# A four-batch adaLN, attention and expert-adapter layer on one core: set-up of the weights and of the first rows rewritten, 64 matmuls put first on TensorE

## The reference, cut to what matters

```python
mod = (silu(c) @ wmod).reshape(4, 6, 1, -1)
sa, ca, ga, sb, cb, gb = (mod[:, i] for i in range(6))
ga = (2 * (ga >= 0) - 1) * max(abs(ga), 0.25)          # gb the same
h = layernorm(x) * (1 + ca) + sa
x = x + ga * attention(h)      # layernorm(h)*gamma+beta -> q, k, v -> causal softmax -> o_proj, + h
h = layernorm(x) * (1 + cb) + sb
x = x + gb * ffn(h)            # silu(gate) * up, 704 wide, with rank-16 adapters of the top 2 of 8 experts
```

## Time and profile before

| | us |
|---|---|
| median of 3 executions | 689.21 (688.83 to 689.48) |
| the profiled execution | 688.73 |
| its span, first to last instruction | 686.9 |
| TensorE matmul busy | 652.9 (95%) |
| VectorE, GpSimd, ScalarE busy | 474.2, 377.4, 356.7 |

### The profile page before, as it was taken

One profiled execution on the slowest core, in us unless ns is written; L12 is line 12 of the kernel. 1 busy time (PEld: TensorE's weight loads), 2 busy tenths in 40 slices (PEclk: granted clock), 3 DMA queues, 4 the chain that ended last, 5 costly groups with the idle time before them and its releaser, 6 DMA issues.

```text
span 686.9 us, 10710 instructions
## 1 busy us (share of the span) xinstructions
PE 652.9 (95%) x3772; PEld 558.8 (81%) x3772; DVE 474.2 (69%) x1146; ACT 356.7 (52%) x642; POOL 377.4 (55%) x473
## 2 busy tenths in 40 slices
PE   4869999999999999999999999999999999999996
PEld 3559987888879987888878897798888998788885
DVE  5997678478886677658976767747987657637323
ACT  4635455546455546465455446564454546654543
POOL 3785345538577236647576516654765635543644
PEclk9989999999999999999999999999999999999999
DMA  8300020000000020000000001000000000000000
GB/s 311 122 1 1 1 62 0 1 2 31 0 2 31 1 62 0 1 1 32 0 1 32 1 1 62 0 1 18 15 1 1 32 1 1 0 1 1 31 0 32
DMA packets 14054, 15.45 MB, mean 22 GB/s; under 512 B 1328, under 2 KB 12720, under 8 KB 14000
## 3 DMA queue, kind: packets, MB, share of 16 engines
q1 hardware_dynamic: 14000, 14.76, 6.4%
HBM read 10.57 MB, written 4.19 MB: 21 GB/s over the span
## 4 chain that ended last, share of the span: by engine, by line
PE 82%; DVE 12%; issue 2%; POOL 2%; DMA 1%; ACT 1%; DVEq 0%; SPq 0%
PE ps L1263 76%; PE ps L1272 6%; DVE xr L856 2%; DVE hid L1103 1%; DVE rstd L829 1%; DVE zb L844 1%; DMA xs<-in_L_attn_x 1%; DVE xT_lo L890 1%; POOL ring_lo L469 1%; DVE mv L836 1%; DVE tr_full L856 1%; ACT act_s L709 1%; DVE zb L927 0%; DVE stat L841 0%; DVE nr_a L827 0%
## 5 line engine op out<-in xcount | busy, mean ns | idle before, releaser
L469 POOL TENSOR_TENSOR ring_lo<-hid,ring_hi 128x512 fp32r<-128x512 f32 x144 | 189.3, 1319 | 115.9 <-ACT ring_hi L717 115.2
L1103 DVE TENSOR_TENSOR hid<-act_s,ps 128x512 f32<-128x512 f32 x120 | 81.9, 684 | 82.0 <-ACT act_s L709 81.4
L709 ACT ACTIVATE act_s<-ps 128x512 f32<-128x512 f32 x120 | 71.7, 597 | 123.0 <-PE ps L1263 122.4
L717 ACT ACTIVATE ring_hi<-hid 128x512 fp32r<-128x512 f32 (+1 forms) x144 | 90.3, 627 | 16.2 <-DVE hid L1101 8.7
L461 POOL TENSOR_TENSOR xT_lo<-tr_full,xT_hi 128x512 fp32r<-128x512 f32 x28 | 35.9, 1297 | 33.5 <-ACT xT_hi L588 33.5
L1263 PE MATMUL ps<-wdT_hi,ring_hi 128*128 128x256 f32 x192 | 53.6, 285 | 0.0
L1263 PE MATMUL ps<-wdT_lo,ring_hi 128*128 128x256 f32 x192 | 53.2, 282 | 0.0
L1263 PE MATMUL ps<-wdT_hi,ring_lo 128*128 128x256 f32 x160 | 45.2, 282 | 0.0
L1263 PE MATMUL ps<-tm_hi,bgT_hi 128*128 128x512 f32 x96 | 39.5, 411 | 5.7 <-DVE hid L1103 5.7
L1263 PE MATMUL ps<-vv_hi,pT_hi 128*128 128x256 f32 x144 | 43.3, 301 | 0.0
L476 POOL TENSOR_TENSOR xr<-xr,y_gb 128x256 f32<-128x256 f32 x31 | 22.1, 739 | 34.2 <-DVE y_gb L1138 34.2
(11 more groups left out here) (229 smaller groups left out, 2026.4 us busy)
## 6 DMA issues: line engine op xcount, KB each, us to landing
xs<-in_L_attn_x SPq DMA_DIRECT2D x4, 1024.0 KB, 5.6
out<-xr SPq DMA_DIRECT2D x7, 512.0 KB, 3.0
s_mod<-in_L_wmod SPq DMA_DIRECT2D x1, 1024.0 KB, 8.8
s_qkvT<-in_L_attn_qkv SPq DMA_DIRECT2D x1, 768.0 KB, 10.3
s_wg<-in_L_ffn_Wg SPq DMA_DIRECT2D x1, 704.0 KB, 7.4
s_wu<-in_L_ffn_Wu SPq DMA_DIRECT2D x1, 704.0 KB, 8.6
s_wd<-in_L_ffn_Wd SPq DMA_DIRECT2D x1, 640.0 KB, 7.3
s_mod<-in_L_wmod SPq DMA_DIRECT2D x1, 512.0 KB, 6.9
```

The source lines that it names most:

```text
L469: pool.tensor_sub(ring[1][:, place(n), :], hid[:, n % HID, :], ring[0][:, place(n), :].bitcast(fp32)).then_inc(h_lo.sem, 1)
L709: nc.scalar.activation(act_s[:, n % 2, :], ps[:, 2 * (n % 2), :], ACT.Silu).then_inc(silu_ready.sem, 1)
L717: nc.scalar.activation(ring[0][p0:P, place(n), :], hid[p0:P, n % HID, :], ACT.Copy).then_inc(h_hi.sem, 1)
L1103: V.tensor_mul(hid[:, n % HID, :], act_s[:, n % 2, :], ps[:, 2 * (n % 2) + 1, :]).then_inc(h_ready.sem, 1)
```

## The change

1. **Loads.** x of batch 0 comes in two transfers. `wmod` comes as shifts and scales of the first norm (512 KB), the gates' columns in two transfers (256 KB each), and, after `qkv` and `o_proj`, the rest. Weights land in float32 buffers (`raw`) which lie where their low halves come to lie; the low half overwrites its own source.
2. **First rows.** VectorE alone makes all eight: four before the gates, four put one by one between the steps of its own Newton chain for tiles 0 to 3. A second Newton chain for tiles 4 to 7 follows, each step waiting for the one before. ScalarE applies the normalisation (`first_normalise`).
3. **Gates.** All batches' gates are made once, as 16 columns of 128 numbers: `mod_row` (products with c as the stationary side), a copy, `mod_turned` (transposes), five small VectorE operations, a spread over 128x2048 on ScalarE, and products with the identity. The gate operations in the bodies go.
4. **GpSimd's queue.** `values_weight` and its low half, the 8 residuals of batch 0, then all twelve weight subtractions, then body 0, which starts with the Newton steps `LN2_A`.
5. **ScalarE's queue.** One weight copy stands in the set-up between its other work, three among the query copies, and eight in body 0 (`BODY_HIGH`): three after the exponentials of tile 3, one after those of tile 4, two after 5 and two after 6.
6. **TensorE's queue.** 64 bf16 matmuls of 128x128 whose result nobody reads stand first. One more modulation product stands between the second transposes and the queries.

```diff
@@ set-up of the pieces @@
+        SPLITS = [(("wg", "wu"), *flat("wgT", k, k + 1)) for k in range(KT)]
+        SPLITS += [(("wu",), *flat("wuT", k, k + 1)) for k in range(KT)]
+        SPLITS += [(("a",), *flat("aT", 0, 2)), (("wr",), s_wr[:, :, :], wrT[0], wrT[1]), (("bd",), *flat("bdT", 0, D)),
+                   (("bg",), *flat("bgT", 0, FP)), (("bu",), *flat("buT", 0, FP)),
+                   (("wd",), *flat("wdT", 0, FT // 2)), (("wd",), *flat("wdT", FT // 2, FT)), (("ad",), *flat("adT", 0, FT))]
+        WEIGHT_STEPS = len(SPLITS)
+        EARLY_HIGH = 4
+        BODY_HIGH = {3: (4, 5, 6), 4: (7,), 5: (8, 9), 6: (10, 11)}
+        MOD_BANKS = (0, 1, 2, 3, 7, 2, 3, 7)
+        MOD_JOBS = (("scale", 0), ("gate", 0), ("scale", 1), ("gate", 1), ("gate", 2), ("gate", 3), ("scale", 2), ("scale", 3))
@@ gpsimd @@
+            def weight_low(j):
+                _, src, hi, lo = SPLITS[j]
                 pool.wait_ge(weight_hi, j + 1)
-                pool.tensor_sub(lo, src, hi.bitcast(fp32)).then_inc(done, 1)
+                ins = pool.tensor_sub(lo, src, hi.bitcast(fp32))
+                if j in (W_D_END, W_AD):
+                    link(ins)
+                    ins = pool.memset((wdT if j == W_D_END else adT)[1][0:FREST, FT - 1, :].bitcast(fp32), 0.0)
+                ins.then_inc(weight_lo, 1)
...
             pool.wait_ge(product_hi, 2)
-            pool.wait_ge(gates_done.sem, gates_done.at(0, 0))
+            pool.wait_ge(mod_copied, 2)
             values_weight(0)
             values_weight_low(0)
             pool.wait_ge(wvo_lo.sem, wvo_lo.at(0, 0))
+            for i in range(NT):
+                pool.wait_ge(first_step, FIRST_ROWS[i])
+                residual(0, i)
+            for j in range(WEIGHT_STEPS):
+                weight_low(j)
...
             def body(b, last):
-                for i in range(NT):
-                    residual(b, i)
+                if b:
+                    for i in range(NT):
+                        residual(b, i)
...
                 for it in range(NEWTON):
                     newton(b, LN2_A, 0, TC, it)
@@ scalar @@
+            act.wait_ge(gates_made, 1)
+            nc.scalar.activation(gate_spread[:, :, :], gateT[:, :].unsqueeze(2).to_broadcast([P, 2 * KT * B, P]), ACT.Copy).then_inc(gates_spread, 1)
...
+            mod_row(1)
+            modulation(1)
+            modulation(2)
...
+            act.wait_ge(first_shift, 1)
+            for i in range(TC):
+                first_normalise(i)
+            values_weight_high(0)
...
+            modulation(3)
+            modulation(4)
+            modulation(5)
+            act.wait_ge(pads_made, 3)
+            weight_high(0)
+            act.wait_ge(first_shift, 2)
+            for i in range(TC, NT):
+                if i >= TC + 2:
+                    attention_inputs(0, (i - TC - 2,))
+                first_normalise(i)
+            modulation(6)
+            attention_inputs(0, range(KT, KT * NC))
+            modulation(7)
+            queries_values(0, range(4))
+            for j in range(1, EARLY_HIGH):
                 weight_high(j)
...
                     scores_exp(i)
...
+                    if b == 0:
+                        for j in BODY_HIGH.get(i, ()):
+                            weight_high(j)
                     if i == NT - 2:
                         act.wait_ge(rstd_ready.sem, rstd_ready.at(b, LN2_A))
@@ vector @@
+            def first_newton(lo, n):
+                v, a, y = nr_v[:, lo:lo + n], nr_a[:, lo:lo + n], rstd[:, lo:lo + n]
+                for _ in range(NEWTON):
+                    yield lambda: V.tensor_mul(a, y, y)
+                    yield lambda: V.scalar_tensor_tensor(a, a, -0.5, v, ALU.mult, ALU.mult)
+                    yield lambda: V.scalar_tensor_tensor(y, a, 1.5, y, ALU.add, ALU.mult)
...
+            big = [lambda i=i: ln1_centre(0, i) for i in second] + [lambda i=i: first_rows(i) for i in second]
+            settle()
+            for n, small in enumerate(first_newton(0, TC)):
+                mark(small())
+                at = steps[1]
+                if n < len(big):
+                    big[n]()
+                dve.wait_ge(vstep, at)
+            first_shifts(0)
+            for i in second:
+                first_stats(i)
+            moments(second)
+            link(guess(TC, TC, True))
+            for small in first_newton(TC, TC):
+                link(small())
+            first_shifts(TC)
...
-                        if r == 8:
-                            dve.wait_ge(out_ready.sem, out_ready.at(b, -1))
-                            gate(b + 1, 0)
-                            gate(b + 1, 1)
-                        if r == 9:
-                            gate(b + 1, 2)
-                            gate(b + 1, 3)
@@ tensor @@
+            pe.wait_ge(consts_made, 6)
+            for _ in range(64):
+                mm(ps[:, 7, 0:P], identb[:, :], identb[:, :], True, True)
             pe.wait_ge(scb_ready, 1)
+            pe.wait_ge(loaded["mod"], 16)
             modulation(0)
+            pe.wait_ge(loaded["mod_gates"], 16 * KT)
+            mod_row(0)
...
+            mod_turned(0, gates_turned)
...
+            pe.wait_ge(mod_copied, 2)
             attention_transposes(0, 0, [xr[:, i, :] for i in range(TC)])
...
+            modulation(6)
+            pe.wait_ge(mod_copied, 7)
+            attention_transposes(0, 1, [xr[:, i, :] for i in range(TC, NT)])
+            modulation(7)
             pe.wait_ge(product_lo, 1)
...
             queries(0)
```

More of the change, by code:

```diff
@@ L373, in _ @@
+            load("bu", raw["buT"][:, F:FP], Bu[:, FULL:F])
+            for key, dst, src in (("wd", raw["wdT"], Wd), ("ad", raw["adT"], Ad)):
                 load(key, dst[:, 0:FT - 1, :], src[0:(FT - 1) * P, :].rearrange("(j p) n -> p j n", p=P))
@@ L581, in weight_high, with first_normalise @@
             def weight_high(j):
-                key, src, (hi, _) = SPLITS[j]
-                act.wait_ge(loaded[key], 16 * LOADS.get(key, 1))
+                keys, src, hi, _ = SPLITS[j]
+                for key in keys:
+                    act.wait_ge(loaded[key], 16 * LOADS.get(key, 1))
                 nc.scalar.activation(hi, src, ACT.Copy).then_inc(weight_hi, 1)
+            def first_normalise(i):
+                nc.scalar.activation(xr[:, i, :], zb[:, i, :], ACT.Identity, bias=shift[:, i:i + 1], scale=rstd[:, i:i + 1]).then_inc(z_ready.sem, 1)
@@ L586, in tr_high, with mod_row @@
+            def mod_row(h):
+                act.wait_ge(rows_ready, h + 1)
+                nc.scalar.activation(mod_rows[:, 2 * D * h:2 * D * (h + 1)], ps[0:B, ROW_BANKS[h], :], ACT.Copy).then_inc(rows_copied, 1)
+            modulation(0)
+            mod_row(0)
             def tr_high(b, q, dst):
@@ L938, in _ @@
                                    wqk[0][:, :, :].rearrange("p k d -> p (k d)").bitcast(fp32), ALU.mult, ALU.subtract).then_inc(product_lo, 1)
-            for i in second:
-                dve.wait_ge(first_h_pool, i - TC + 1)
-                mark(V.bn_stats(stat[:, i, :], zb[:, i, :]))
-            moments(second)
-            guess(TC, TC).then_inc(first_guess, 1)
-            dve.wait_ge(first_rstd, 1)
-            for i in first:
-                normalise(i, zb, z_ready, xr[:, i, :])
-            dve.wait_ge(mod_copied, 2)
-            gate(0, 1)
-            gate(0, 2)
-            weight_low(W_BG)
             dve.wait_ge(loaded["ln"], 32)
@@ L955, in _ @@
                 attention_low(q)
-            dve.wait_ge(first_rstd, 2)
-            for i in second:
-                normalise(i, zb, z_ready, xr[:, i, :])
-            gate(0, 3)
-            settle()
-            dve.sem_inc(gates_done.sem, 1)
-            weight_low(W_BU_REST)
             attention_scale(0, range(KT, KT * NC))
@@ new lines, in mod_row, with mod_turned @@
+            def mod_row(h):
+                for t, c0 in enumerate(((2, 5), (3, 4))[h]):
+                    for k in range(KT):
+                        last_mm = mm(ps[0:B, ROW_BANKS[h], t * D:(t + 1) * D], scT[:, k, :], s_mod[:, k, c0 * D:(c0 + 1) * D], k == 0, k == KT - 1)
+                last_mm.then_inc(rows_ready, 1)
+            def mod_turned(h, done):
+                pe.wait_ge(rows_copied, h + 1)
+                for q in range(2 * KT):
+                    last_mm = nc.tensor.transpose(ps[:, TURN_BANK, (2 * KT * h + q) * B:(2 * KT * h + q + 1) * B],
+                                                  mod_rows[:, (2 * KT * h + q) * P:(2 * KT * h + q + 1) * P], ident[0:B, 0:B])
+                last_mm.then_inc(done, 1)
@@ L1295, in _ @@
                 last_mm.then_inc(product_ready, 1)
+            pe.wait_ge(loaded["mod_rest"], 16)
+            mod_row(1)
+            pe.wait_ge(gates_spread, 1)
+            modulation(1)
+            modulation(2)
+            mod_turned(1, modT_ready)
+            for job in range(3, 6):
+                modulation(job)
             def transposes(b, q, bank, k, rows):
```

316 lines of the change are left out of this document (116 added, 200 removed).

## The result

| us | before | after |
|---|---|---|
| median (lowest to highest, 4 executions each) | 689.02 (688.75 to 689.48) | 697.96 (697.34 to 698.39) |
| profiled execution, its span | 688.73, 686.9 | 698.03, 696.2 |
| TensorE matmul busy in the span | 652.9 | 662.8 |

The account below looks back on a forecast made before the run. Bound: when the second transposes can start, and any new TensorE hold-up behind 49.15. Terms 1.0 + 6.3 + 2.6 + 1.0 = +10.9 on 688.7 give 699.6, median 700.1; own forecast 697.5 to 703, range 688.5 to 703.

Parts of the forecast that it names:

- first shift: Set-up, VectorE: shift for the first four tiles, made after gates and Newton chain, forecast at 25.5 us.
- second shift: Set-up, VectorE: shift for tiles 4 to 7, Newton steps held by GpSimd's residuals, forecast at 36.9 us.
- second transposes: Set-up, TensorE: behind ScalarE's 4.4 us of work after the second shift, forecast at 41.3 against 40.69.
- start of the values, against before: End of set-up, TensorE: values at 50.2 against 49.15, +1.0; bounds -7.65 and +3.
- guess beside the subtractions: Batch 0 attention, VectorE: root's guess held by GpSimd's subtractions 8 and 9, +2.6; 0 if steps pass freely.
- root and what stands behind it: Batch 0 attention: Newton steps `LN2_A` behind GpSimd's subtractions 10 and 11 delay ScalarE and TensorE, +6.3.
- clock behind that wait: Batch 0 attention: TensorE idles 79.6 to 87.3, then runs 3 us at half clock, +1.0 (0 to 2).
- rival 5: VectorE and GpSimd on SBUF: each waits for the other's whole operation, nothing overlaps, 701.4 us; chance 0.05.
- (3): Set-up as forecast, but batch 0's guess passes freely and the clock does not fall, 696.5 us; chance 0.15.
- (1): Set-up's tiny steps slip between residuals, gaining 7.65, while the late root costs +6.3; say 690.5 us; chance 0.22.
- (2): Batch 0's root costs TensorE under 4 us, less than the set-up saves; 685.5 with full -7.65; chance 0.13.
- (4): Start of kernel: warm-up's clock has fallen again when wanted; no change in time; goes with any other case.

Follow-up runs that it names:

- the last experiment: Changed kernel with root's Newton steps first, copies 7 to 9 earlier, residuals and `values_weight_low` after the second shift, 50 unread matmuls ahead of second transposes: 682.69 us.
- the 110 matmuls: Changed kernel plus 110 unread bf16 matmuls of 128x128 on TensorE in its 7 us wait ahead of the transposes of `zb` in batch 0: 695.47 us.

## Why the prediction was right, point by point

The direction, the mechanism of the main loss and the range held. That the total came so near is in part luck: the set-up was forecast to lose 1.0 and gained 1.4, and more than half of that error was made up by 1.4 us in the later batches, which had been put at nothing. The sizes:

| step | forecast, us | measured, us |
|---|---|---|
| first shift | 25.5 | 24.9 |
| second shift | 36.9 | 32.8 |
| second transposes | 41.3 | 36.83 |
| modulation product between them and the queries | 1.7 | 3.5 |
| start of the values, against before | +1.0 | -1.4 |
| guess beside the subtractions | +2.6 | +2.0 |
| root and what stands behind it | +6.3 | +6.0 |
| clock behind that wait | +1.0 | +1.3 |
| later batches | 0 | +1.4 |
| sum | +10.9 | +9.3 in the span, +8.9 in the medians |

**First shift.** The spread of the gates took 1.91 us (2.0 forecast). `values_weight` held one small VectorE step (1.23 us where its like take 0.15), so its turn was priced about right.

**Second shift.** This is the term that was mis-sized most. The prediction put nine chained steps at "one residual operation, 0.8" each, 7.2 us with 1.45 ahead of them. The chain took 5.2 us from its first step to its last, which the timeline above explains: three steps pass per two GpSimd operations. Rows 4 showed that a lone tiny step is held until GpSimd's operation ends, and that is true of every held step here. What rows 4 could not show is the rate of a chain: it depends on GpSimd's own gaps, and a gap of 0.08 us is enough for a step. Besides, `values_weight_low` came at 27.67 and not at 28.2. The experiments with GpSimd kept silent give the two ends: 1.9 us with nothing beside it, 2.9 with `wvo_lo` alone.

For this the Trainium skill was weighed (page "SBUF — State Buffer", section "Who interferes with whom"). Its rule, that the loser is blocked for the other's whole instruction, holds for each held step in this trace. As a price for the chain, my rival 5 made of it 0.95 us per step. The measured mean is 0.52 (5.2 by ten), so that rival fell, because it had every step meet an operation.

**Second transposes.** The path behind the shift took 4.1 us (32.76 to 36.83; 4.4 forecast). The clock fell in the wait, as assumed. From the transposes to the values it took 10.9 us, not 8.9. The queries ran at full pace, as put (5.6 us); but the modulation product ahead of them is four passes at half pace and not the two that the prediction counted, 3.5 us (38.60 to 42.1) instead of 1.7, and full speed was back only at 42.2, 5 us after work resumed and not 3:

```profile
38.60 3.62 PE L1238 MATMUL ps<-s_mod,s_scb 128*128 128x512 f32 x4
```

That returned most of what the earlier shift had gained: transposes 3.9 us earlier, values 1.4. With the clock kept up by unread matmuls the same stretch takes 8.25. The prediction's lower bound, transposes at 34.0 and values at 41.5 if no step is held and the clock does not fall, is what the last experiment comes to: 33.65 and 41.90.

**The guess.** The two turns that it was forecast to wait were seen: 1.21 and 1.77 us, and the guess took 3.35 us instead of the 0.73 that it took undisturbed. So its own length grew by the 2.6 forecast. What follows it moved by less: the maximum of tile 6 starts at 72.09 instead of 71.52, which with the set-up's lead of 1.4 is +2.0, because before the change VectorE had idled 0.23 ahead of it and the guess had stood 0.3 later.

**The root.** The measured starts 75.12, 77.28 and 79.32 are spaced nearly as forecast (2.2 and 2.0 us, where 2.2 and 2.2 had been put), and the Newton steps took 3.54 us (3.55). The prediction counted guess and root up to the transposes of the exponentials, 8.9 together. In the changed kernel these stand at half speed directly behind the transposes of `zb`, so wait and clock mix. With the 110 matmuls they don't: there they start at 87.19, behind ScalarE's exponentials, against 80.44 before and with a set-up 1.25 ahead. That is 8.0, with 2.0 of it from the guess.

**The clock.** From the transposes of `zb` to the mark at 101.43 the changed kernel takes 16.4 us (before: 79.57 to 93.51, 13.9), and 2.0 of the 2.5 difference are the two groups of transposes at half speed (3.92 against 1.90). But with full speed TensorE would have waited 0.90 and 0.85 for ScalarE in the same place, so net the clock cost 1.3 in the trace, within the bounds of 0 to 2; the medians' 2.5 would lie outside them.

**What was costed at nothing.** The missing gates were worth nothing that could be measured. The 64 matmuls were not either, but not for the reason given: the prediction had them save 0.85 us at best, off the path; in the traces they save 1.8 us on the first product, about 0.8 of it on the path to the second transposes, and it is the clock behind the later wait that hides it. The product had been priced too low here as well. The later batches were not free: +0.4 us in each. A like stretch of each kernel shows where a part of it is, 24 matmuls of 128x512 between one wait and the next transposes. TensorE's timeline before, then after:

```profile
270.81 0.51 PE L1263 MATMUL ps<-tm_hi,bgT_hi 128*128 128x512 f32 x1 [1.33 <-DVE hid L1103]
...
276.39 1.04 PE L1272 MATMUL ps<-ident,zb 128*128 128x128 f32 x8
```
```profile
279.20 0.50 PE L1238 MATMUL ps<-tm_hi,bgT_hi 128*128 128x512 f32 x1 [1.32 <-DVE hid L1088]
...
284.90 1.03 PE L1247 MATMUL ps<-ident,zb 128*128 128x128 f32 x8
```

The same 24 matmuls with no wait among them take 5.58 and 5.70 us, at a granted clock of 1.00 in both. They are slower themselves, by 2%. The experiment with the gates put back shows 5.69, so it is not the gates. Among what is left are the places of the weights and other buffers in SBUF and of the instructions in memory, which the change moved too, and what the other engines do beside these matmuls. None was tried alone, and this cause stays open.

**The rivals.** (3), the guess passing freely, fell by the 1.21 and 1.77. (1) had tiny steps that slip in between, and one in three did; but the set-up then gave 1.4 and not 7.65, since the other steps were held and the clock fell. (2) needed that 7.65 and a root that costs TensorE under 4 us; the root cost 6.0. (4) had the warm-up lapsed when it is wanted; it had not: the first product took 1.96 us with it and 3.77 without. What lapsed was the clock in the wait from 30 to 37, which the 64 matmuls can't reach; its forecast of no change in the time held all the same.

**The signs.** Of those named, GpSimd's two subtractions ahead of the 128x4 steps, ScalarE's idle stretch (7.12 us) and TensorE's wait at a clock of 0.5 behind it came. The second transposes near 41 did not (36.83, little above the 36 that was to count against the forecast), nor did steps of 0.7 to 0.9 us beside the residuals: the held ones took 0.57 to 0.65, and every third 0.16 or 0.17.

## What to carry to other kernels

One-off work that is moved into an in-order queue is priced by what stands behind it, not by its amount alone: moving two of twelve subtractions from ahead of the root to behind it gave back 9.75 us, with all twelve still done. A chain of tiny VectorE steps that others wait for should run while GpSimd is silent: one semaphore wait on GpSimd was worth 3.8 us by the medians, more than the chain's own 2.2, of which the trace puts 0.4 to TensorE's clock behind the wait and leaves the rest open. Where TensorE has to wait on the critical path, matmuls whose result nobody reads can go into that wait: they gave 2.2 and 2.5 us there by the medians (2.2 and 1.3 in the traces). At the start of the kernel they gave nothing that the time shows. And an unchanged time is no proof that something is off the path: only the trace without the 64 matmuls showed that the path is longer without them.

## What the runs showed that had not been expected

- A chain of ten VectorE steps of 128x4 beside a GpSimd that works back to back took 5.2 us, against 1.9 alone; per step it alternates between 0.17 and about 0.6 us, as GpSimd's own dependencies leave a gap or not.
- Steps with one source are held as well: 1.21 and 1.77 us for a `TENSOR_SCALAR` of 128x4 that takes 0.17 with GpSimd idle.
- Behind a wait of 6.7 or 7.0 us the granted clock was 0.50 for 5 us of nearly unbroken work in the changed kernel's profile. It differed between kernels with the same set-up. In the profile of the one with the gates put back the clock fell at about 32.9, in the wait, and was back at 39.7; in that with 110 matmuls in turn 8 it fell at 32.4 and was back only at 42.5. Their values start at 46.22 and 47.90; 0.6 of this they had already at the transposes. One execution of each can't tell changes of under 1.7 us in that place.
- A granted clock of 1.00 does not say that TensorE runs at full pace: without the 64 matmuls the first modulation product took 3.77 us at 1.00, with them 1.96 at 1.00.
- The same matmuls in the same order and at the same granted clock ran 2% slower in one stretch of the changed kernel (5.70 against 5.58 us for 24), with no wait among them.
